# Attention with 16 heads in three matmul passes: the projected value tiles spread over the four steps of an image

## The reference

```
xn  = layer_norm(x, norm_w, norm_b)
q, k, v = xn @ q_w + q_b, xn @ k_w + k_b, (xn @ v_w + v_b) * mask     16 heads of 32 features
att = softmax over m of (q[n] . k[m] + (1 - mask) * -1e6)             per head, 512 x 512
y   = att @ v
h   = silu(layer_norm(y) * (1 + scale) + shift) @ out_w + out_b       scale, shift: silu(emb) @ emb_w + emb_b
x   = x + h
```

## Time and profile before

| | us |
|---|---|
| median of 3 runs | 2758.56 (2758.4 to 2762.62) |
| the profiled execution | 2760.54 |
| its span, first to last instruction | 2758.7 |
| mean granted clock of PE | 0.985 |
| attention phase within the span | about 1523 |
| steps of a steady image (image 7) | 23.94, 22.13, 20.29, 24.06 |

### The profile page before, as it was taken

The page is one execution under the profiler, slowest core; times in us unless marked ns, Lnnn a source line. Parts: engine busy times, 40 slices in busy tenths (PEclk is TensorE's granted clock), DMA queues, the critical chain, the costliest instruction groups (busy, mean ns, idle before and its releaser), DMA issues. The chain is left out here.

```text
span 2758.7 us, 43942 instructions
## 1 busy us (share of the span) xinstructions
PE 2656.1 (96%) x13890; PEld 1946.4 (71%) x13890; DVE 1797.8 (65%) x3216; ACT 1253.5 (45%) x2097; POOL 1348.3 (49%) x634
## 2 busy tenths in 40 slices
PE   6999999999999999999999899999999999999997
PEld 4666666666665666666664678888888888888886
DVE  5666666666666666666655677666666777676664
ACT  3555555555555555555555332333333333333332
POOL 1566666666665666666663233434433333334332
PEclk8999999999999999999999899999999999999999
DMA  6656665666566656665665411111111111111110
GB/s 140 94 83 97 98 102 79 98 98 101 80 98 101 102 79 98 101 98 80 98 100 143 150 36 47 50 50 50 50 50 50 50 46 50 38 39 46 34 31 31
DMA packets 114915, 211.44 MB, mean 77 GB/s; under 512 B 12408, under 2 KB 14508, under 8 KB 114876
## 3 DMA queue, kind: packets, MB, share of 16 engines
q1 hardware_dynamic: 78012, 143.81, 22.6%
q10 hardware_dynamic: 36864, 67.13, 18.4%
HBM read 74.87 MB, written 34.18 MB: 40 GB/s over the span
## 5 line engine op out<-in xcount | busy, mean ns | idle before, releaser
L929 DVE TENSOR_REDUCE negmax<-max_bank 128x1 f32<-128x512 f32 x1024 | 681.8, 687 | 324.1 <-PE max_bank L537 322.5
L800 ACT ACTIVATE probs<-exp_bank 128x512 f32<-128x512 f32 x1024 | 584.2, 597 | 495.0 <-PE exp_bank L552 463.5
L299 POOL TENSOR_TENSOR probs_sum<-probs_sum,probs 128x2048 f32<-128x2048 f32 x124 | 571.6, 4610 | 57.7 <-ACT probs L800 53.9
L299 POOL TENSOR_TENSOR probs_sum<-probs 128x2048 f32<-128x2048 f32 x63 | 288.5, 4579 | 529.7 <-ACT probs L800 529.7
L552 PE MATMUL exp_bank<-q_stack,k_stack 100*128 100x512 f32 x1024 | 425.8, 427 | 21.6 <-ACT probs L800 21.4
L537 PE MATMUL max_bank<-k_stack,q_stack 98*128 98x512 f32 x1024 | 418.6, 412 | 8.2 <-DVE negmax L929 8.1
L552 PEld LDWEIGHTS exp_bank<-q_stack,k_stack 100*128 100x128 f32 x1024 | 192.6, 190 | 159.2 <-ACT probs L800 79.3
L537 PEld LDWEIGHTS max_bank<-k_stack,q_stack 98*128 98x128 f32 x1024 | 193.0, 190 | 114.3 <-issue 52.5
L1567 POOL TENSOR_TENSOR sT_lo<-silu,sT_hi 128x512 fp32r<-128x512 f32 x128 | 173.1, 1372 | 176.7 <-DVE sT_hi L1683 176.7
L563 PE MATMUL y_bank<-probs,v_sb 128*32 128x512 f32 x2048 | 250.4, 607 | 0.0
L1332 PE MATMUL b_work<-ident,area 128*128 128x128 f32 x1536 | 192.6, 280 | 22.6 <-DVE area L1652 15.4
(11 more groups left out here) (197 smaller groups left out, 5304.4 us busy)
## 6 DMA issues: line engine op xcount, KB each, us to landing
q_stack<-q_stage ACTq DMA_DIRECT2D x128, 256.0 KB
k_stack<-k_stage ACTq DMA_DIRECT2D x128, 256.0 KB
x_sb<-in_x SPq DMA_DIRECT2D x16, 1024.0 KB, 5.6
q_stack<-q_stage SPq DMA_DIRECT2D x64, 256.0 KB
k_stack<-k_stage SPq DMA_DIRECT2D x64, 256.0 KB
yT_scratch<-y_stage SPq DMA_DIRECT2D x64, 256.0 KB
area<-yT_scratch SPq DMA_DIRECT2D x16, 1024.0 KB, 5.3
area<-in_x SPq DMA_DIRECT2D x64, 256.0 KB, 2.7
```

Source lines behind the costliest of these rows:

```text
L299: eng.tensor_tensor(probs_sum[:, :, :], so_far, probs[:, mt, :, :], ALU.add).then_inc(probs_added, 1)
L800: act.activation(probs[:, mt, j, :], exp_bank[k % 2][:, :], ACT.Exp).then_inc(exp_done, 1)
L929: dve.tensor_reduce(negmax[:, m:m + 1], max_bank[m % 2][:, :], AXX, ALU.max, negate=True).then_inc(max_done, 1)
```

## The change

`QUARTERS` becomes one table for each step. Value tile 1 moves from step 3 of the image before to step 0 (slots 4 and 5), tile 2 stays in step 0 (slots 10 and 11), tile 3 moves from step 0 to step 1 (slots 4 and 5), tile 0 stays in step 3, now in slots 13 to 15. In steps 0 and 1 the quarters of k move from slots 4 to 7 to slots 6 to 9, and with them ScalarE's and VectorE's parts and the DMAs. The transposes of x move from slots 8, 9, 11, 13 to 10, 11, 13, 14. In the prologue value tile 1 is not made any more. The order of the bank's uses follows; the loads of the condition weights are placed anew. The number of instructions stays the same.

```diff
--- before.py
+++ after.py
@@ -216,34 +216,37 @@
         def uses_of(g, last):
             u = []
             if not last or g < NG - 2:
-                u += ["q", "k"]
+                u += ["q"]
+            if g < 2:
+                u += [f"v{2 * g + 1}"]
+            if not last or g < NG - 2:
+                u += ["k"]
             if g == 0:
                 u += ["v2"]
             if g == 1 and not last:
-                u += [f"x{tt}" for tt in range(TT - 1)]
-            if g == NG - 1 and not last:
-                u += ["v0"]
+                u += [f"x{tt}" for tt in range(TT - 2)]
             if not last or g < NG - 1:
                 u += ["m"]
+            if g == 1 and not last:
+                u += [f"x{tt}" for tt in range(TT - 2, TT)]
             if last and g == NG - 2:
                 u += ["film0a", "film0b"]
             if last and g == NG - 1:
                 u += ["film0c", "film1a", "film1b", "film1c"]
-            if g == 1 and not last:
-                u += [f"x{TT - 1}"]
-            if g == 0:
-                u += ["v3"]
             if g == NG - 1 and not last:
-                u += ["v1"]
+                u += ["v0"]
             return u
 
-        FIRST_USES = [f"x{tt}" for tt in range(TT)] + ["q0", "k0", "q1", "k1", "v0", "v1", "m"]
+        FIRST_USES = [f"x{tt}" for tt in range(TT)] + ["q0", "k0", "q1", "k1", "v0", "m"]
         USES = sum(len(uses_of(g, False)) for g in range(NG))
         assert USES % 2 == 0
 
 
-        QUARTERS = {"q": (0, 1, 2, 3), "k": (4, 5, 6, 7), "v": (8, 9, 10, 10), "v'": (13, 14, 15, 15)}
-        X_TURNS = (8, 9, 11, 13)
+        QUARTERS = ({"q": (0, 1, 2, 3), "v1": (4, 4, 5, 5), "k": (6, 7, 8, 9), "v2": (10, 10, 11, 11)},
+                    {"q": (0, 1, 2, 3), "v3": (4, 4, 5, 5), "k": (6, 7, 8, 9)},
+                    {"q": (0, 1, 2, 3), "k": (4, 5, 6, 7)},
+                    {"q": (0, 1, 2, 3), "k": (4, 5, 6, 7), "v0": (13, 14, 15, 15)})
+        X_TURNS = (10, 11, 13, 14)
         MAX_TURN = 12
 
         FILM_TURNS = {(NG - 2, 13): (0, 0), (NG - 2, 14): (0, 1), (NG - 2, 15): (1, 0), (NG - 1, 0): (1, 1)}
@@ -264,6 +267,14 @@
 
             n = len(FIRST_USES) + sum(len(uses_of(h, last)) for h in range(g)) + uses_of(g, last).index(what)
             return n, b * USES + n
+
+        def quarters_of(g, last):
+
+            return [(name, slots) for name, slots in QUARTERS[g].items() if name in uses_of(g, last)]
+
+        def values_of(g, last):
+
+            return [(int(name[1]), slots) for name, slots in quarters_of(g, last) if name[0] == "v"]
 
         def step_of(b, g):
             return b * NG + g
@@ -390,16 +401,12 @@
                 if not last or g < NG - 1:
                     n_b, n_g = (b, g + 1) if g + 1 < NG else (b + 1, 0)
                     shift_rows(n_b, n_g, use(b, g, "m", last)[1] + 1)
-                if last and g == 0:
-                    sp.wait_ge(work_full, use(b, 0, "v3", last)[1] + 1)
-                    for part in (1, 2):
+                if last and g == 1:
+                    for part in (1, 2, 3):
                         load_emb(0, part)
-                if last and g == 1:
-                    load_emb(0, 3)
-                    for part in (0, 1):
-                        load_emb(1, part)
+                    load_emb(1, 0)
                 if last and g == 2:
-                    for part in (2, 3):
+                    for part in (1, 2, 3):
                         load_emb(1, part)
                 if g == 2 and not last:
 
@@ -663,16 +670,14 @@
                 bias_quarter("v", sums_bank, kt)
             pe.wait_ge(cols_done, 3)
             pe.wait_ge(condT_done, 1)
-            first_v = {}
             for m in range(SLOTS):
                 max_scores(0, 0, m, first=True)
-                if 5 <= m < 5 + 2 * KT:
-                    tile, kt = divmod(m - 5, KT)
-                    if kt == 0:
+                if 5 <= m < 5 + KT:
+                    if m == 5:
                         pe.wait_ge(w_split, 3)
-                        n = FIRST_USES.index(f"v{tile}")
-                        first_v[tile] = take_bank((n, n))
-                    project_quarter("v", tile, first_v[tile], kt, kt == 0, kt == KT - 1)
+                        n = FIRST_USES.index("v0")
+                        first_v = take_bank((n, n))
+                    project_quarter("v", 0, first_v, m - 5, m == 5, m == 4 + KT)
             n = FIRST_USES.index("m")
             transpose_max(0, 0, (n, n))
             pe.wait_ge(bias_done, 2)
@@ -709,16 +714,8 @@
                         film_product(0, half, use(b, NG - 2, "film0" + "ab"[half], last), c)
                     if last and g == NG - 1 and k in FILM_COLUMN_TURNS:
                         film_columns(0, use(b, g, "film0c", last), FILM_COLUMN_TURNS.index(k))
-                    for name, slots in QUARTERS.items():
-                        if name in "qk":
-                            if last and g >= NG - 2:
-                                continue
-                            what, tile, u = name, (g + 2) % NG, name
-                        elif g == 0 or (g == NG - 1 and not last):
-                            tile = (2 if g == 0 else 0) + (name == "v'")
-                            what, u = "v", f"v{tile}"
-                        else:
-                            continue
+                    for name, slots in quarters_of(g, last):
+                        what, tile = (name, (g + 2) % NG) if name in "qk" else ("v", int(name[1]))
                         for kt in range(KT):
                             if slots[kt] != k:
                                 continue
@@ -726,7 +723,7 @@
 
                                 pe.wait_ge(work_read, use(b, 1, f"x{TT - 1}")[1] + 1)
                             if kt == 0:
-                                banks[name] = take_bank(use(b, g, u, last))
+                                banks[name] = take_bank(use(b, g, name, last))
                             project_quarter(what, tile, banks[name], kt, kt == 0, kt == KT - 1)
                     if g == 1 and not last and k in X_TURNS:
                         tt = X_TURNS.index(k)
@@ -835,8 +832,7 @@
                     act.wait_ge(cond_in, DMA)
                     act.activation(cond_rows, cond_rows, ACT.Silu).then_inc(cond_act, 1)
             act.wait_ge(cols_done, 2)
-            for mt in range(2):
-                mask_value(0, mt, FIRST_USES.index(f"v{mt}"))
+            mask_value(0, 0, FIRST_USES.index("v0"))
 
             def exp_slot(b, g, e, first=False):
                 exp(b, g, e, first)
@@ -850,7 +846,7 @@
                     if not (first and g == 0 and k < LAG):
                         exp_slot(*exp_of(b, g, k), first and g == 0)
                     for what in "qk":
-                        if k == QUARTERS[what][-1] and (not last or g < NG - 2):
+                        if k == QUARTERS[g][what][-1] and (not last or g < NG - 2):
 
                             p_b, p_g = (b, g + 1) if g + 1 < NG else (b + 1, 0)
                             act.wait_ge(stack_in[p_g], DMA * STACK_DMAS * (p_b + 1))
@@ -863,12 +859,9 @@
                         tt = X_TURNS.index(k)
                         static, number = use(b, 1, f"x{tt}")
                         high_of_x(tt, number, static)
-                    if k == 12 and (g == 0 or (g == NG - 1 and not last)):
-                        mt = 2 if g == 0 else 0
-                        mask_value(b if g == 0 else b + 1, mt, use(b, g, f"v{mt}", last)[1])
-                if g == 0 or (g == NG - 1 and not last):
-                    mt = 3 if g == 0 else 1
-                    mask_value(b if g == 0 else b + 1, mt, use(b, g, f"v{mt}", last)[1])
+                    for mt, slots in values_of(g, last):
+                        if k == min(slots[-1] + 2, SLOTS - 1):
+                            mask_value(b if g < NG - 1 else b + 1, mt, use(b, g, f"v{mt}", last)[1])
 
             for g in range(NG):
                 step(0, g, first=True)
@@ -1029,9 +1022,7 @@
                 if m == 10:
                     dve.wait_ge(v_bias_done, 1)
                     add_value_bias(0, 0, n, n)
-                if m == 14:
-                    add_value_bias(0, 1, n + 1, n + 1)
-            split_shift(0, 0, n + 2, n + 2)
+            split_shift(0, 0, n + 1, n + 1)
 
             def step(b, g, last=False):
                 has_next = not last or g < NG - 1
@@ -1041,14 +1032,14 @@
                         for m in maxima(k):
                             maximum(n_b, n_g, m)
                     for i, what in enumerate("qk"):
-                        if k == QUARTERS[what][-1] + 1 and (not last or g < NG - 2):
+                        if k == QUARTERS[g][what][-1] + 1 and (not last or g < NG - 2):
                             low_of(what, (g + 2) % NG, use(b, g, what, last)[0], high_count(b, g, i))
                     if g == 1 and not last and k - 1 in X_TURNS:
```

(11 more changed lines are left out.)

## The result

The changed kernel takes 2838.55 us (median of 4, 2835.95 to 2844.17), the kernel before 2759.9 beside it: a ratio of 1.0281, 95% interval 1.0262 to 1.0300. It is slower by about 79 us. Forecast were 2831 us and a range of 2800 to 2866.

A forecast was written before the change was run, and what follows sets the result against it. PE, busy 96%, bounds the kernel, with k's DMA landing setting steps 0 and 1. Middle images +3.95 us 14 times (55), first 3.3, last 7.7, together +66, clock +6: 2831 us against the median 2758.56, range 2800 to 2866.

The forecast's parts named there:

- What set the steps: Steps 0 and 1: k's transfers land 26.3 us after the step begins, PE waits; +2.15 and +3.95 us an image.
- The price of a tile by slots held: A value tile costs 2.80 us in full slots, 2.15 in slots 8 to 11, 1.63 in slots 12 to 15.
- The clock: Start of step 2, after step 1's tail: PE's clock falls more often, 1.5 us each, one in three more, +6 us.
- The ends: First and last image: +3.3 us with the prologue, +7.7 us for the last, none gained in its step 3.
- The moved loads of 1 MB: Last image, two loads moved to the end of step 1: 0, or up to 3 us if they meet other traffic.
- rival B: Steps 0 and 1: k lands in time, no DMA wait; +2.1 us an image, +32, 2791 us; chance 0.11.
- My bound for step 1 without the wait: Step 1: PE's own time if no transfer is waited for, 24.8 us, bounds 23.4 and 24.9.
- A: Tiles fill idle time, mostly step 1's 1.55 us; -1.55 us an image, -23, 2735 us; chance 0.04.
- C: Shift rows late in slot 3, +31 us; clock falls in nearly every image, +20; up to 2882 us; chance 0.15.

The follow-up runs named there:

- e8: Changed kernel with one of k's three stack transfers cut to 2 KB in images 1 to 14, nothing moved: 2812.22 us, ratio 1.0195 to the kernel before.
- e2: Changed kernel with value tile 2 of step 0 in slots 13, 14, 15, 15 in place of 10, 10, 11, 11: 2818.59 us, ratio 1.0216.
- e3: Changed kernel with four more matmuls, whose result nothing reads, in slots 13 to 15 of step 0 of every image: 2821.33 us, ratio 1.0223.
- e9: Kernel before with one of k's three stack transfers cut to 2 KB, as a control: 2766.2 us, ratio 1.0034.
- e11: Changed kernel with k in slots 6, 7, 8, 8, transposes of x in 9, 10, 11, 13, value tile 2 in 13, 14, 15, 15: 2792.28 us, ratio 1.0119.
- e4: Kernel before with k of steps 0 and 1 in slots 6 to 9, transposes of x in 10, 11, 13, 14, value tiles untouched: 2824.43 us, ratio 1.0238.
- e1: Changed kernel with the k quarters of steps 0 and 1 in slots 6, 6, 7, 7 in place of 6, 7, 8, 9: 2836.88 us, ratio 1.0282.

## Why the prediction was right, point by point

**What set the steps.** Forecast: k's first transfer 18.0 us into steps 0 and 1, landing 8.3 later, PE waiting there some 32 times. Measured: 17.88 in step 0 (in step 1 18.0 where it starts without a wait, e8), about 8.2, 31 times. From max matmul to max matmul (at 732.27, 758.18, 785.71) step 0 is 25.9 (forecast 26.1), step 1 27.5, and 26.0 without the clock's fall (e2 and e3; forecast 26.1). PE's delay is 0.43 us behind step 0 (forecast 0.5) and 1.05 behind step 1 (forecast 1.3 to 2). Steps 2 and 3 are 20.4 and 21.8 (forecast 20.3 and 21.9). The price of a tile by slots held: step 3 gave 2.19, forecast 2.15.

**The clock** was mis-sized: "one in three more, +6". It fell in every image, and at the start of step 1, behind the tail of step 0, where the prediction had named the tail of step 1, at 1.54 us each (e3): 16 falls are 24.6 us, less the 4.5 that the kernel before spent on its three. That is 14 us above the term, and more than the 8 by which the forecast was short. Without the falls an image grew by 3.51 us where 3.95 were forecast, 6 us less over the 14 images; so that the total came so near is in part luck, two errors of opposite sign.

**The ends.** Image 0 with the prologue is 3.6 us longer (forecast 3.3), the last one 10.2 (94.99 against 84.77, forecast 7.7); each has one of the 16 falls in it. The last image's step 2 goes from 22.39 to 26.36: 2.60 of that is the wait for k at its start (1547.21 to 1550.15, less 0.34), which the forecast booked in step 1, and 1.37 is the low clock after it (0.71 from 1550.15 on, 0.85 before). The moved loads of 1 MB are issued from 1547.37, after k's transfers, and PE waits for none of them; the forecast had them at nothing.

**What the sum left hidden.** It booked 3.95 us an image to a landing and kept rival B, the places alone, at 2.1. With the landing out of the way, 2.70 of the 5.05 us are left (e8); the full landing adds 0.81 (e3 against e8), the clock 1.54 (after against e3). So a little over half of the loss is not the wait and what comes with it: 1.9 us are the places of the tiles, which rival B priced at 2.1, and 0.8 the late transpose of x, which it had at nothing. The wait with its fall of the clock is 2.35. My bound for step 1 without the wait (24.8) held (24.88). The last transpose of x stands in slot 14 now: step 2's first q quarter waits for it, seen only once the DMA wait is gone. The wait in slot 11 of step 1 (0.35 us in every steady image) was in the 24.8, unnamed.

**The rivals.** A (faster) fell as its row said: the idle 1.55 us of step 1 grew to 1.73 in place of being filled. B did not hold for the kernel, but is what e8 makes of it: 2812 against its 2791, the difference being that 0.8 us in each image, and the first and last image, which keep the wait (2.5 and 9.8 us longer than before). Of C the clock came true, the shift rows did not: they land up to 5.8 us after their issue (3.3 before) and no exp matmul waited. The 2.0 us and 436 GB/s of the Trainium skill, DMA: Bandwidth & Descriptors, "Anatomy of one DMA", are given there for DMAs that GpSimd issues; the prediction did not say so, and these are issued by ScalarE and SyncE. Taken for them all the same, they give an estimate of 3.8 us for k's three transfers. The trace disagrees: 8.2 us, at 125 GB/s and a full share (755 to 756).

**Not settled:** the 0.3% of e9; what the spread alone costs (e11 has a wait of its own); why just these transfers run at 125 GB/s when their first microsecond shows 238; what keeps the last image's clock low.

## What to carry to other kernels

Fill costs what its slot leaves: the same twelve matmuls cost 2.80 us in full slots (2.75 measured in step 1 of e8), 2.15 in half-full ones, 1.63 in a tail paced by another engine, so even out idle time, not matmul counts. A tile that feeds a DMA chain has a due time, its issue plus the chain alone (8.2 us here) against the first reader; read it off the trace before moving the tile later, and remember that other work of PE hides the time in which an engine issues DMAs (1.35 us on ScalarE, bare in e4). When a wait is removed, look at once for what stands behind it: e1 and e8 each had another wait ready behind it.

## What was not expected of the hardware

PE's clock was granted at 0.50 for 3.41 us once in each image, after a wait of only 0.43 us, and that cost 1.54 us, three times the wait. The wait alone does not do it: in e2 it is 0.93 us and the clock stays at 1.00, with the slots ahead of it filled; in e8 the slots are as bare as in the changed kernel, the wait is gone, and the clock falls in one steady image. Four matmuls an image without a purpose (0.23 us each at full clock), put where PE idles, took the falls away at no cost: 17 us of 2838.
